# Mixing branch and first router as one pipeline; norm and fold placed beside the collecting of expert rows

## What is computed

```python
# layer 0, mixing branch (8 heads of 32)
qkv = xn @ Wqkv;  q, k, v = split(qkv)
q = softmax(q, axis=-1) * 32**-0.5         # over the 32 features of a head
k = softmax(k, axis=tokens)
context = einsum('bhnd,bhne->bhde', k, v)
out = einsum('bhde,bhnd->bhne', context, q) @ Wout
x = x + gnn(xn) + layernorm(out) * gamma
# layer 0, experts
xt = layernorm(x)
probs = softmax(xt @ Wr + br)              # 8 experts, the best two are kept
xe = layernorm(xt) * ln_g[e] + ln_b[e]     # and so on, the experts' outputs weighted and added to x
# layer 1
xn = layernorm(x)                          # the graph branch uses W[r] and W[r] folded with attn_src, attn_dst
```

## Time and profile before

| | |
|---|---|
| median of 3 runs | 4262.99 us (4262.08 to 4263.6) |
| profiled execution, its own time | 4303.09 us |
| its span | 4301.4 us |
| mean granted TensorE clock, share of full | 0.846 |
| busy: TensorE, VectorE, ScalarE, GpSimd | 3272.8, 2092.9, 772.1, 1123.9 us (76, 49, 18, 26%) |

### The profile page before, as it was taken

One profiled execution on the slowest core, in us unless ns is written; L12 is line 12 of the kernel. 1 busy time (PEld: TensorE's weight loads), 2 busy tenths in 40 slices (PEclk: granted clock), 3 DMA queues, 4 the chain that ended last, 5 costly groups with the idle time before them and its releaser, 6 DMA issues. The chain is left out here.

```text
span 4301.4 us, 49813 instructions
## 1 busy us (share of the span) xinstructions
PE 3272.8 (76%) x14155; PEld 2416.5 (56%) x14156; DVE 2092.9 (49%) x4998; ACT 772.1 (18%) x1519; POOL 1123.9 (26%) x1178
## 2 busy tenths in 40 slices
PE   3899799979986245999819964676767677669998
PEld 2677588868865233888714534454545455545555
DVE  7999823323323640000046634666665766653333
ACT  0222122222222111332202310000000000022222
POOL 4810000000000224000040034666666666400000
PEclk9999999989998656999959976677777777769999
DMA  2722255444400014212124223444434344210000
GB/s 77 269 110 95 103 131 133 107 129 126 128 9 0 0 44 127 73 55 81 47 59 120 115 92 101 113 121 111 120 108 120 107 122 120 79 58 8 8 15 30
DMA packets 306806, 383.82 MB, mean 89 GB/s; under 512 B 40199, under 2 KB 249840, under 8 KB 303248
## 3 DMA queue, kind: packets, MB, share of 16 engines
q1 hardware_dynamic: 240016, 218.38, 16.3%
q0 software_dynamic: 50992, 146.13, 12.1%
q10 hardware_dynamic: 15696, 18.09, 1.3%
HBM read 270.97 MB, written 111.53 MB: 89 GB/s over the span
## 5 line engine op out<-in xcount | busy, mean ns | idle before, releaser
L2218 POOL DMA_INDIRECT relations_or_ring<-relation_rows,table_row x280 | 275.4, 983 | 468.7 <-SPq L1992 300.0
L496 PE MATMUL counts_acc<-onehot_lo,onehot_key 128*128 128x400 bf16 x2000 | 361.6, 336 | 46.7 <-DVE onehot_key L478 46.7
L475 DVE TENSOR_SCALAR onehot_lo<-node_ids,source_lo 128x800 bf16<-128x800 int16 x1000 | 360.2, 471 | 0.0
L496 PEld LDWEIGHTS counts_acc<-onehot_lo,onehot_key 128*128 128x128 bf16 x2000 | 267.9, 139 | 144.6 <-DVE onehot_key L478 86.4
L2358 PE MATMUL att_po<-att_near,att_onehotT 128*128 128x64 f32 x1568 | 240.7, 307 | 78.8 <-issue 72.6
L709 PE MATMUL agg_agg<-xn_or_ring,agg_slab 128*128 128x257 f32 x1250 | 278.5, 382 | 25.7 <-DMA agg_slab<-edge_counts 25.7
L709 PE MATMUL agg_agg<-x_gnn,agg_slab 128*128 128x257 f32 x1250 | 277.3, 381 | 19.1 <-DMA agg_slab<-edge_counts 19.1
L2218 POOL DMA_INDIRECT tables_or_ring<-relation_rows,table_row x252 | 250.4, 994 | 153.4 <-issue 71.3
L2218 POOL DMA_INDIRECT xn_or_ring<-relation_rows,table_row x252 | 250.4, 994 | 124.0 <-issue 71.3
L2358 PEld LDWEIGHTS att_po<-att_near,att_onehotT 128*128 128x128 f32 x1568 | 224.7, 222 | 88.0 <-issue 86.9
L709 PEld LDWEIGHTS agg_agg<-xn_or_ring,agg_slab 128*128 128x128 f32 x1250 | 238.5, 191 | 61.6 <-DMA agg_slab<-edge_counts 25.8
(11 more groups left out here) (430 smaller groups left out, 5355.3 us busy)
## 6 DMA issues: line engine op xcount, KB each, us to landing
agg_slab<-edge_counts SPq DMA_DIRECT2D x50, 1600.0 KB, 7.9
edge_counts<-counts_out SPq DMA_DIRECT2D x100, 400.0 KB, 2.3
relation_rows<-tables_or_ring SPq DMA_DIRECT2D x25, 1056.0 KB, 3.9
att_targets<-targets SPq DMA_DIRECT2D x28, 896.0 KB
wide_w<-L_ffn_W ACTq DMA_DIRECT2D x14, 1024.0 KB
expert_rows_in<-blank_rows POOLq DMA_DIRECT2D x34, 256.0 KB
expert_rows_out<-blank_rows POOLq DMA_DIRECT2D x33, 256.0 KB
ffn_xin<-expert_rows_in SPq DMA_DIRECT2D x31, 256.0 KB, 2.9
```

The costliest lines, as they stand in the source:

```text
L475: nc.vector.tensor_scalar(oh_lo[:, k, j, :], c.nodes[:, 0:LO], lo[:, ds(at + j, 1)], None, ALU.is_equal)
L496: mm = nc.tensor.matmul(acc[:, k, h, 0:HALF_LO], oh_key[:, k, :, j], oh_lo[:, k, j, h * HALF_LO:(h + 1) * HALF_LO], start=False, stop=Fals ...
L2218: self.nc.gpsimd.indirect_dma_start(self.slots[p % RING][:, j, :], None, self.rows_of, bass.IndirectOffsetOnAxis(ap=self.c.row[:, n:n + 1] ...
```

## The change

`linear_context` takes over the softmax of q: the product q stands beside v in one PSUM bank (`pvq`), VectorE reduces and subtracts each head's greatest, ScalarE takes exp, VectorE sums, inverts and scales; v's copy stands between. VectorE's loop is written out.

```diff
@@ linear_context, VectorE and ScalarE, per tile
-                    nc.scalar.copy(tile_of(q, t), pqk[:, b, 0:D]).then_inc(q_out, 1)
-                    nc.scalar.activation(ek[:, b, :], pqk[:, b, D:2 * D], ACT.Exp).then_inc(k_exp, 1)
+                    nc.scalar.activation(ek[:, b, :], pk[:, b, 0:D], ACT.Exp).then_inc(k_exp, 1)
+                    act.wait_ge(q_less, t + 3)
+                    nc.scalar.activation(tile_of(q, t), tile_of(q, t), ACT.Exp).then_inc(q_exp, 1)
...
                     v.wait_ge(summed, t + 3)
+                    link(nc.vector.tensor_reduce(m, pvq[:, b, D:2 * D].rearrange("p (h d) -> p h d", d=32), AX, ALU.max))
+                    nc.vector.tensor_tensor(heads, pvq[:, b, D:2 * D].rearrange("p (h d) -> p h d", d=32), wide,
+                                            ALU.subtract).then_inc(q_less, 1)
                     v.wait_ge(ctx_done, t + 1)
-                    nc.vector.tensor_copy(vv[:, b, :], pv[:, b, 0:D]).then_inc(v_out, 1)
-                tiles(v, NT, step)
+                    nc.vector.tensor_copy(vv[:, b, :], pvq[:, b, 0:D]).then_inc(v_out, 1)
+                    v.wait_ge(q_exp, t + 1)
+                    link(nc.vector.tensor_reduce(m, heads, AX, ALU.add))
+                    link(nc.vector.reciprocal(m, m))
+                    link(nc.vector.scalar_tensor_tensor(out=heads, in0=heads, scalar=scale, in1=wide,
+                                                        op0=ALU.mult, op1=ALU.mult))
```

`head_softmax`, `turn`, `statistics`, `normalize`, `route` and `fold_attention` go. Items 3, 4 and 6 (without `load`) become one block, `mix_and_route`, with the tiles in four groups (7, 6, 6, 6). The lists of the engines, cut to their order:

```diff
+def mix_and_route(g, name, c, q, fold, gamma, xt, wr, br, logits, choice):
...
+    ends = [7, 13, 19, NT]
...
+                flip_q(0)                       # TensorE
+                mix(0)                          # per tile: flip_q(t + 1), multiply(t)
+                for k in range(ng):
+                    if k + 1 < ng:
+                        mix(k + 1)
+                    router(k)                   # per tile: flip_x(t) waits for normed, choose(t - 1)
+                choose(NT - 1)
...
+                keep_q(0)                       # ScalarE
+                mix(0)                          # per tile: keep_q(t + 1), keep_h(t)
+                mixed.root(act, 0)
+                for k in range(ng):
+                    if k + 1 < ng:
+                        mix(k + 1)
+                    first.root(act, k)
+                    if k + 1 < ng:
+                        mixed.root(act, k + 1)
+                    act.wait_ge(ready, k + 1)
+                    for t in groups[k]:
+                        normalise(t)
+                        if t:
+                            keep_x(t - 1)
+                keep_x(NT - 1)
+                second.root(act, 0)
+                choice.exponents(act)
+                act.wait_ge(ready2, 1)
+                for t in range(NT):
+                    nc.scalar.activation(xt[:, t, 0:D], xt[:, t, 0:D], ACT.Identity, bias=back2[:, t:t + 1],
+                                         scale=second.rstd(t)).then_inc(normed2, 1)
...
+                measure(0)                      # VectorE; per tile: wait h_kept, bn_stats
+                mixed.moments(v, 0)
+                for k in range(ng):
+                    if k + 1 < ng:
+                        measure(k + 1)
+                    add(k)                      # per tile: two chained scalar_tensor_tensor, bn_stats
+                    first.moments(v, k)
+                    if k + 1 < ng:
+                        mixed.moments(v, k + 1)
+                    less_mean(first, back, k, ready)
+                    if k:
+                        measure_again(k - 1)    # per tile: wait normed, bn_stats
+                measure_again(ng - 1)
+                second.moments(v, 0)
+                less_mean(second, back2, 0, ready2)
+                v.wait_ge(routed, NT)
...
+                choice.choose(v)
```

(The remarks after `#` in this listing name engines and steps; they are not in the code.) The six router loads join `mix_weights`, which ScalarE issues at the head of the second `aggregate`. `collect_tokens` takes over "ln3" and the fold: `attn` and the fold's 64 products run at its start, the four copies after tile 12, and VectorE's loop becomes:

```diff
+                def finish(k):
+                    norms.invert(v, k)
+                    for t in range(norms.ends[k - 1] if k else 0, norms.ends[k]):
+                        nc.vector.tensor_scalar(xn[:, t, 0:D], x[:, t, :], norms.mean(t), norms.rstd(t),
+                                                ALU.subtract, ALU.mult).then_inc(normed, 1)
...
                         v.wait_ge(added, 2 * t + k + 1)
+                    norms.take(t, x[:, t, :])
+                    if t + 1 in norms.ends:
+                        norms.moments(v, norms.ends.index(t + 1))
+                    if t in norms.ends:
+                        finish(norms.ends.index(t))
+                    if t == NT // 2:
+                        keep_fold()
+                finish(len(norms.ends) - 1)
```

More of the change, by code:

```diff
@@ L564, in _ @@
                     sp.wait_ge(s, 16 * (NCW // 2) + 16)
[L567 to L598, removed]
@@ L1730, in _ @@
                 for m in range(KT):
[L1731 removed]
+                    ins = nc.vector.tensor_scalar(m_out[:, m, :], pk[:, m, 0:D], inv[:, m:m + 1], None, ALU.mult)
                 ins.then_inc(masked, 1)
[L1735 removed]
+def mix_and_route(g, name, c, q, fold, gamma, xt, wr, br, logits, choice):
     nc = g.nc
[L1738 removed]
+    ne = logits.shape[2]
+    ends = [7, 13, 19, NT]
+    groups = [range(a, b) for a, b in zip([0] + ends, ends)]
+    ng = len(groups)
@@ new lines, in choose, with mix @@
+                def choose(t):
+                    pe.wait_ge(x_kept, t + 1)
+                    for k in range(KT):
+                        mm = nc.tensor.matmul(pl[:, t, :], xtT[:, t % 2, k, :], wr[:, k, :],
+                                              start=(k == 0), stop=(k == KT - 1))
+                    mm.then_inc(routed, 1)
+                def mix(k):
+                    for t in groups[k]:
+                        if t + 1 < NT:
+                            flip_q(t + 1)
+                        multiply(t)
@@ new lines, in less_mean, with measure_again @@
+                def less_mean(norms, out, k, sem):
+                    at = slice(norms.ends[k - 1] if k else 0, norms.ends[k])
+                    norms.invert(v, k)
+                    nc.vector.scalar_tensor_tensor(out=out[:, at], in0=norms.few[:, 3, at], scalar=-1.0,
+                                                   in1=norms.few[:, 2, at], op0=ALU.mult, op1=ALU.mult).then_inc(sem, 1)
+                def measure_again(k):
+                    for t in groups[k]:
+                        v.wait_ge(normed, t + 1)
+                        second.take(t, xt[:, t, 0:D])
@@ L3162, in build_program @@
             ne = 8
[L3163 to L3174 removed]
+            gates = gates0
             slots = g.sb(own, "slots0", [P, 2, NT], I32)
```

406 lines of the change are left out of this document (194 added, 212 removed).

## The result

The changed kernel takes 4140.2 us (median of four runs, 4138.7 to 4143.2) beside 4263.3 us of the kernel before (four runs, 4262.1 to 4266.2): a ratio of 0.9711, 95% interval 0.9694 to 0.9728, 123.1 us less. The forecast was 4141. Its profiled execution took 4138.91 us (span 4137.3), so here the profile stands at the median; that of before stood 40 us above its own. One execution among all that follow, of experiment 5, took 4401 us at a lower mean clock (0.784 against 0.855 to 0.861) and is left out of its ratio.

A forecast was written before the change was run, and what follows sets the result against it. It took the replaced stages to be stretches in which mostly one engine works while the others wait. Savings of 83.3 (mixing) and 39.2 us (collecting, norm, fold) sum to 122.5: 4263.0 becomes 4140.5, say 4141; range 4112 to 4170.

The forecast's parts named there:

- The context loop: Softmax of q in the context loop: hidden by TensorE, costing nothing in the loop and 0.9 us for the last tile.
- mix_and_route: New mixing stage: engines take turns group by group in written order; 131.6 us for 214.9, 83.3 us less.
- Rival 3: Mixing stage: better overlap, VectorE's own work sets the end; 92.4 us instead of 129.5, 4104 us in all; chance 0.06.
- mix(0) is taken hot: Start of the mixing stage: the first group's mixing runs at full clock, 1.08 us a tile.
- The price named for this case: Start of the mixing stage: if mix(0) runs cold, up to 6.5 us / 2 more.
- the third long turn: Mixing stage, from 63.4 to 93.1 us: router(1) 7.4, mix(3) 9.6, last bn_stats 0.9, add(2) 11.8.
- Rival 2: Mixing stage: TensorE stays at the cold clock, 7 to 21 us more, about 4160 us; chance 0.17.
- about 65 us: Collecting: GpSimd's issues stay at 950 ns with 0.3 between them, in a block of some 65 us.
- Rival 1: Collecting: VectorE's scalings hold up GpSimd's issues, 10.3 us longer; 4151 us in all; chance 0.12.
- The forecast tail of 6.4 us: Behind the last collected pair: 4.1 us of remaining norm work and some 2.3 us for the block's end.
- collecting: Collecting, norm and fold: 6.4 us remain of 45.6 for norm and fold, 39.2 us less.
- The 40 us of the profile of before: Profiled execution 40.1 us over the runs' median, assumed outside the changed stages; if in proportion, 1.1 us less gain.

The follow-up runs named there:

- experiment 5: Changed kernel with VectorE measuring group k+1 behind add(k), and TensorE and ScalarE mixing two groups ahead; ratio 0.9655 to the kernel before, stage 96.7 us.
- experiment 4: Changed kernel with v's copy moved behind the whole softmax chain in the context loop; ratio 0.9711 to the kernel before.
- experiment 2: Changed kernel with one line moved: VectorE measures group k+1 behind add(k) instead of ahead; ratio 0.9642 to the kernel before, stage 106.4 us.
- experiment 7: Changed kernel with four unused matmuls behind the last one of the context stage; ratio 0.9700 to the kernel before, stage 126.9 us.
- experiment 1: Changed kernel with collecting, norm and fold put back as in the kernel before, mixing part kept; ratio 0.9795 to the kernel before.
- experiment 8: Changed kernel with 64 satisfied waits ahead of VectorE's collecting loop; ratio 0.9728 to the kernel before.
- experiment 11: Changed kernel with measurement moved behind add(k), mixing two groups ahead, four unused matmuls and ten row buffers; 3907.6 us, ratio 0.9613 to the kernel before.
- experiment 9: Changed kernel with the collecting's moments taken once and all 25 tiles scaled behind the loop; 3947.0 us, ratio 0.9709 to the kernel before.
- experiment 3: Changed kernel with all scalings of the collected rows behind the collecting loop; ratio 0.9727 to the kernel before.
- experiment 10: Changed kernel with the fold in a block of its own behind the collecting; 3956.9 us, ratio 0.9734 to the kernel before.
- experiment 6: Changed kernel with ScalarE instead of VectorE scaling the collected rows; ratio 0.9736 to the kernel before.
- experiment 12: The kernel of experiment 11 run again, on a fourth chip; 3907.9 us, ratio 0.9608 to the kernel before.

## Why the prediction was right, and where it was not

**The context loop: right.** 0 us in the loop and 0.9 for the last tile were forecast; the window ends 1.1 us later. VectorE's work was sized at 2.5 us a tile and took 57.2 / 25 = 2.3. Experiment 4 shows the slack that the prediction argued for.

**mix_and_route: right, by the turns.** Forecast from the start of the block 19.3 for the first measurement, then 32.5, 63.4, 93.1 and 105.5; measured from TensorE's first transposes 20.5, then 33.3, 63.5, 91.6 and 104.2. The first work on the slots comes 85.4 us earlier, 83.3 were forecast. Experiments 2 and 5 show that it came out so for the reason given: with the order changed and the work kept, the stage goes from 130.1 to 106.4 and 96.7 us. Rival 3 had put 92.4 us for a block bound by VectorE; that is what experiment 5 approaches, so it was the right limit for another written order.

**Failed step: "mix(0) is taken hot".** The 0.97 of the earlier trace rows is a mean over a gap of 2.2 us in which TensorE ran nothing; the clock with which the next work starts was not read. The fall lies at the end of that same row, as finer windows of the trace of before show:

```profile
1357.50:1358.40 0.90, 0.00 (x0) 0.00 (x0) 0.70 (x1) 0.00 (x0) 0.00 (x0) 1.00 0.00 0
1358.40:1359.00 0.60, 0.00 (x0) 0.00 (x0) 0.60 (x1) 0.00 (x0) 0.00 (x0) 0.55 0.00 0
```

In the kernel after it fell at the same place, between 1358.5 and 1359.3, and the new stage ran its first 6.7 us at 0.53. The price named for this case (6.5 / 2 us) was right or somewhat high: experiment 7 gained 3.2 us on the kernel after, 2.2 on the 129.1 us that experiments 1, 4 and 8 took for the same stage. The sum hardly felt it: the rest of the first turn took 2.0 us less than its terms (20.5 - 3.2 against 19.3), and the third long turn came out at 28.1 us, where 29.7 were forecast.

**Rival 2, a TensorE that stays cold, did not come.** The router's matmuls never left 0.50, but in mix(2), which began at 1401.15, the clock rose after 4.5 us: three tiles at half clock and three at full, as its term had it, 9.3 us for 9.6. mix(3) rose too, at 1433.7.

```profile
1401.10:1405.60 4.50, 4.50 (x14) 3.57 (x15) 0.43 (x1) 1.12 (x3) 0.00 (x0) 0.50 0.00 0
1405.60:1410.50 4.90, 4.88 (x25) 3.91 (x23) 1.71 (x4) 2.68 (x8) 0.00 (x0) 0.91 0.00 0
```

**Failed step: the collecting block "about 65 us".** It was 71.0. Rival 1 saw a longer block coming, but with another cause and size: 10.3 us by held-up issues. GpSimd's last issue came 5.8 us later than before (67.2 us after the first, for 61.4). Of that, longer issues are 1.1 us (1.6 in experiment 11 beside 9, where nothing else held them), and 4.7 us are the two waits for a free buffer behind the slow stretch, 4.0 and 1.3 less the usual 0.3 each. The Trainium skill's rule ("SBUF — State Buffer", section "SBUF: two separate sides"), taken as a lock for the whole of each scaling, is not borne out in that size: the four issues of the kernel after that lie wholly beside scalings took 1.01, 0.95, 0.95 and 1.02 us, and in experiment 3 issues of 1.06 stand beside pairs and bn_stats alone. Whether the scalings ran in a two-port mode at all no row tells; they followed each other at 0.33 us, no faster than bn_stats. The slow stretch could not be read from the trace of before. The forecast tail of 6.4 us was 5.3. Together 34.7 us saved for 39.2.

**The cancelling.** The terms were +2.1 (mixing), -4.5 (collecting) and 4.2 us between the slots and the collecting, which nobody forecast and which the traces of unchanged code vary by (568.8 to 573.1 us in the kernels before and after and experiments 1 to 8). That the time came out within 1 us of the forecast is partly luck; the two terms by themselves were within 3% and 12%.

**The 40 us of the profile of before** were assumed to lie outside the changed stages: right as far as the traces tell, which differ by 39.8 us behind the tables.

**What stays open** is the slow stretch. Eight traces have it (the kernel after and experiments 2 to 8), all from chips on which the kernel before takes 4263 to 4291 us; experiment 1, of such a chip, has the old block and none. Four traces have none, all from chips at 4064 to 4068 us; one of them, experiment 10, has the moments and five buffers. The shift of the list (8), the scalings' place (3) and their engine (6) don't take it away. Whether the chip, the ten buffers, the moments or the fold decides is not settled, since no kernel with all of the new block and five buffers ran on a chip at 4064 to 4068 us, and none of 9 to 12 on one of the others.

## To carry to other kernels

When several engines share a pipeline whose order is written by hand, write the turns down group by group from single prices before asking what each engine's sum is: here the sums of work allowed some 92 us (an estimate; 96.7 were reached) and the order cost 130, and moving one line gave back 24 of the difference. Add up an issue queue and its consumer with their buffers, too: a consumer busy 46 of 71 us stalls a queue as soon as it loses 12 us in one place and only five buffers stand between. And compare stages, not totals, when chips differ by more than the change is worth.

## What the hardware showed

- **Chips differ by a tenth in one stretch of the same code**, and by 5% in the whole. Up to the collecting the traces agree within some 10 us; from the tables to the end the kernel after takes 2005.1 us, experiments 9 to 12 take 1818 to 1819 us on two other chips. GpSimd's issues there have the same duration, but other idle time. First the kernel after from 2426 us on, then experiment 9:

```profile
L2213 POOL DMA_INDIRECT relations_or_ring<-relation_rows,table_row x252 | 251.8, 999 | 145.8 <-issue 71.0 <-PE att_acc L2390 41.7 <-DMA xn_or_ring<-L_ffn_ln_b_t 33.1
```

```profile
L2213 POOL DMA_INDIRECT relations_or_ring<-relation_rows,table_row x252 | 251.6, 998 | 76.8 <-issue 74.6 <-PE att_acc L2390 2.1
```

  The waits for TensorE's sums and for transfers, 75 us in this group, are 2 us on the other chip. Which resource is slower there wasn't tried.
- **Small chained VectorE operations can go 1.4 us apart for 12 us and more** instead of 0.2, each of them still 0.17 us long, beside GpSimd's indirect DMAs.
- **The mean clock of a gap isn't the clock the next stage starts with**: in the kernel after still 1.00 one us after the last matmul of the context stage, 0.50 by the end of the gap of 1.8 us, and 0.53 in the 6.7 us of work behind it. In experiment 7 it fell during matmuls, behind gaps of only 0.7 and 0.8 us.
- ScalarE's `Identity` with bias and scale per partition took 585 to 602 ns for 128x256 and followed each other at 0.50 us (25 in 12.4).
